# The tail of layer 3's query and key splits moved from VectorE to GpSimd, and the planner's tables replaced

## What is computed

```
for each of 4 layers:
    x = x + gate * out(self_attention(norm(x) * scale + shift))
    x = x + gate * out(cross_attention(norm(x) * scale + shift, context))
    x = x + gate * mlp(norm(x) * scale + shift)
```

## Time and profile before

| | before |
|---|---|
| median of 3 runs | 2908.7 us (2907.26 to 2917.39) |
| the profiled execution | 2916.84 us |
| its span, first to last instruction | 2915.0 us |
| instructions | 47676 |
| mean granted TensorE clock | 0.976 of full speed |
| DVE busy | 65% |
| ACT busy | 49% |
| POOL busy | 20% |

### The profile page before, as it was taken

The page is one execution under the profiler, slowest core; times in us unless marked ns, Lnnn a source line. Parts: engine busy times, 40 slices in busy tenths (PEclk is TensorE's granted clock), DMA queues, the critical chain, the costliest instruction groups (busy, mean ns, idle before and its releaser), DMA issues. The chain is left out here.

```text
span 2915.0 us, 47676 instructions
## 1 busy us (share of the span) xinstructions
PE 2728.5 (94%) x15136; PEld 1351.8 (46%) x15136; DVE 1893.7 (65%) x4209; ACT 1425.8 (49%) x2579; POOL 590.3 (20%) x999
## 2 busy tenths in 40 slices
PE   8999999999989999999988888898999999999899
PEld 5444344335544424334455566656645323224456
DVE  5977388642574783866344889668974884885621
ACT  3455635574445583566644444333221674785441
POOL 2110001131331110331125323411020010112510
PEclk9999999999999999999998999999999999999899
DMA  6333122433452312233066516521420322123621
GB/s 207 69 104 107 41 72 71 112 89 98 144 172 53 114 51 67 91 115 95 22 186 186 167 50 195 146 85 60 147 60 1 116 60 52 45 61 108 183 92 38
DMA packets 268153, 286.78 MB, mean 98 GB/s; under 512 B 70665, under 2 KB 207243, under 8 KB 267275
## 3 DMA queue, kind: packets, MB, share of 16 engines
q1 hardware_dynamic: 256651, 282.28, 33.0%
q0 software_dynamic: 11264, 1.46, 0.3%
HBM read 167.43 MB, written 114.72 MB: 97 GB/s over the span
## 5 line engine op out<-in xcount | busy, mean ns | idle before, releaser
L1570 ACT ACTIVATE probs<-ring_b 128x512 f32<-128x512 f32 (+1 forms) x1728 | 921.8, 599 | 457.9 <-PE ring_b L1429 359.9
L1748 DVE TENSOR_REDUCE row_max<-ring_a 128x1 f32<-128x1024 f32 x512 | 602.0, 1218 | 151.7 <-PE ring_a L1385 150.9
L1429 PE MATMUL ring_b<-q_ring,k_ring 100*128 100x512 bf16 x1536 | 526.8, 381 | 10.5 <-ACT probs L1570 2.8
L1385 PE MATMUL ring_a<-k_ring,q_ring 96*128 96x512 bf16 x1536 | 450.1, 383 | 27.9 <-DVE row_max L1748 16.1
L1462 PE MATMUL ring_c<-probs,v_and_ones 128*17 128x512 f32 x3072 | 402.0, 599 | 1.8 <-ACT probs L1570 1.2
L1745 DVE CUSTOM_DVE_ANT_0 w_mlp<-ring_a,w_mlp 128x1024 bf16<-128x1024 f32 x256 | 302.1, 1222 | 49.6 <-PE ring_a L1385 48.4
L1868 POOL CAST neg_max_parts<-neg_max 16x128 bf16<-16x128 f32 x112 | 37.6, 336 | 1392.1 <-ACT neg_max L1564 1141.3
L1429 PEld LDWEIGHTS ring_b<-q_ring,k_ring 100*128 100x128 bf16 x1536 | 145.7, 97 | 349.9 <-issue 241.5
L1385 PEld LDWEIGHTS ring_a<-k_ring,q_ring 96*128 96x128 bf16 x1536 | 135.5, 98 | 250.5 <-issue 153.6
L1485 PE MATMUL ring_b<-h_feat,w_mlp 128*128 128x512 f32 x512 | 230.3, 595 | 1.4 <-ACT h_feat L1541 0.8
L1497 PE MATMUL ring_a<-w_mlp 128*128 128x256 f32 x1024 | 226.1, 380 | 5.0 <-DVE w_mlp L1803 2.4
(11 more groups left out here) (143 smaller groups left out, 3346.4 us busy)
## 6 DMA issues: line engine op xcount, KB each, us to landing
q_ring<-scr_q SPq DMA_DIRECT2D x128, 384.0 KB, 4.3
scr_q<-split SPq DMA_DIRECT2D x64, 384.0 KB, 2.6
k_ring<-scr_k SPq DMA_DIRECT2D x64, 384.0 KB, 5.0
scr_q<-split SPq DMA_DIRECT2D x64, 256.0 KB, 3.0
scr_out<-out_stage SPq DMA_DIRECT2D x128, 128.0 KB, 2.5
scr_out<-out_stage SPq DMA_DIRECT2D x64, 256.0 KB, 2.4
h_feat<-scr_out SPq DMA_DIRECT2D x56, 256.0 KB
reciprocals<-scr_recip SPq DMA_DIRECT2D x56, 256.0 KB
```

The source lines that it names most:

```text
L1385: last = mm(ps[:, half * BLOCK:(half + 1) * BLOCK], q[0:PARTS, h, t * P:(t + 1) * P], k_view(g)[0:PARTS, h, half * BLOCK:(half + 1) * BLOC ...
L1429: last = mm(ps[:, :], k_view(g)[0:ROWS, h, s.kt * P:(s.kt + 1) * P], q[0:ROWS, h, q0:q0 + BLOCK], start=not g.masked, stop=True)
L1570: f(PT[0:n, s.pt, :], ps[0:n, :], ACT.Exp, **kw).then_inc(b_evac, 1)
L1748: v.tensor_reduce(NM[:, s.nm, s.u:s.u + 1], ps, AX.X, ALU.max).then_inc(a_evac, 1)
```

## The change

Three things. In layer 3 (`TAILS = (3,)`) a rotated split becomes two steps: `rotate` (PE and the first four DVE instructions) and `tail` (three GpSimd instructions, the same arithmetic), with a semaphore from DVE to POOL and one from POOL to whoever waits for the split. The splits of the context's keys stay as they were. The DMAs of the maxima stay on POOL's queue, as before. And all tables that set the order (`RANK`, `SECOND`, `LATER`, `REACH`, `DELAY`) have new numbers, so that the order changes in all layers, mostly by a few places.

```diff
-REACH = dict(PE=0.0, ACT=0.0, DVE=0.05, POOL=0.0, SP=0.2)
-DELAY = (7.5, 100)
+REACH = dict(PE=0.0, ACT=0.05, DVE=0.0, POOL=0.8, SP=0.2)
+DELAY = (7.5, 7.5)
-    tk=(10.1, 0.1, -12, 9.9),
+    tk=(-7, -12, -12, -11),
...
+TAILS = (3,)
...
-        d = yield do("split", ([("PE", 0.264 if ck else 0.86)] if rope else []) + [("DVE", (2.08 if rope else 0.84) if ck else 4.3 if rope else 1.79)],
-                     after=[s], ring="a" if rope else None, counts=["split_n"], of=s, rope=rope, l=l)
+        if rope and l in TAILS and not ck:
+            t = yield do("rotate", [("PE", 0.86), ("DVE", 2.55)], after=[s], ring="a", counts=["turned_n"], of=s, l=l)
+            d = yield do("tail", [("POOL", 3.5)], after=[t], counts=["tail_n"], of=s, turned=t, l=l)
+        else:
+            d = yield do("split", ([("PE", 0.264 if ck else 0.86)] if rope else []) + [("DVE", (2.08 if rope else 0.84) if ck else 4.3 if rope else 1.79)],
+                         after=[s], ring="a" if rope else None, counts=["split_n"], of=s, rope=rope, l=l)
...
+                        if s.kind == "rotate":
+                            v.tensor_copy(parts[:, 0, :], r).then_inc(turned, 1)
...
+                elif s.kind == "tail":
+                    f = s.of
+                    r = RAW[:, f.raw, 0:f.width]
+                    parts = SPLIT[:, f.split, :, 0:f.width]
+                    pool.wait_ge(turned, s.turned.turned_n + 1)
+                    link(g_.tensor_tensor(out=r, in0=r, in1=parts[:, 0, :], op=ALU.subtract))
+                    link(g_.tensor_copy(parts[:, 1, :], r))
+                    g_.tensor_tensor(out=parts[:, 2, :], in0=r, in1=parts[:, 1, :], op=ALU.subtract).then_inc(tail_done, 1)
```

More of the change, by code:

```diff
@@ L283 @@
 RANK = dict(
[L284 to L295, removed]
-    tk=(10.1, 0.1, -12, 9.9),
-    tk_s=(-0.5, 6.1, -9.2, -5.2),
-    win_f=(-6, -12, -4, 0),
-    win_s=(10.5, 8.5, 7.5, 6.5),
-)
-REACH = dict(PE=0.0, ACT=0.0, DVE=0.05, POOL=0.0, SP=0.2)
-DELAY = (7.5, 100)
[L303 to L306, removed]
+    init=(13.7, 1.2, -5.8, 1.9),
+    mod=(10.8, 10.8, -3.2, 11.1),
+    prep=(12.3, -9, -2.9, -2.9),
+    out=(0, -10, -8, -10),
+    ctx=(8.3, -6.7, 10.3, -6.7),
+    load=(24, 1.8, -10, 1.8),
+    cross_f=(-6.9, 10.8, 2.1, 3.1),
+    cross_s=(7.7, 3.8, 8.9, 12.9),
+    mlp=(-1, -1, -1, 0),
+    self_f=(-3, 24, 23, 20),
+    self_pv=(22, 24, 22, 24),
+    self_s=(-11, 1.1, -12, 3.1),
+    tk=(-7, -12, -12, -11),
+    tk_s=(6.7, -0.9, -12, 6.7),
+    win_f=(5.8, 8.5, -2.9, -8),
+    win_s=(6.2, 0.5, 4.5, -4.4),
+)
+REACH = dict(PE=0.0, ACT=0.05, DVE=0.0, POOL=0.8, SP=0.2)
+DELAY = (7.5, 7.5)
+SECOND = dict(init=24, mod=-23, prep=-3, out=3, ctx=16, load=-11, cross_f=20,
+              cross_s=15, mlp=-11, self_f=-4, self_pv=12, self_s=-1, tk=-13, tk_s=-3,
+              win_f=-22, win_s=20)
+LATER = (-9, -5.5, -6, -28)
 FILL_ONE = 0.11
+TAILS = (3,)
 def rank_of(kind, l, b, blk):
@@ L996, in blocks_kernel, with split_ended @@
         xn_ready, ctxn_ready = sem("xn_ready"), sem("ctx_norm_ready")
-        split_done = sem("split_done")
+        split_done, turned, tail_done = sem("split_done"), sem("rotated"), sem("tail_done")
+        def split_ended(eng, d):
+            if d.kind == "tail":
+                eng.wait_ge(tail_done, d.tail_n + 1)
+            else:
+                eng.wait_ge(split_done, d.split_n + 1)
         scr_in = [sem(f"scratch_written_{i}") for i in range(SPLITS)]
@@ L1153, in _ @@
                         elif r.kind == "scratch":
-                            sp.wait_ge(split_done, r.done.split_n + 1)
+                            split_ended(sp, r.done)
                         elif r.kind == "ctx_put":
@@ L1163, in _ @@
                     d, s = s.done, s.of
-                    sp.wait_ge(split_done, d.split_n + 1)
+                    split_ended(sp, d)
                     for j, parts in SCRATCH[s.which[-1]]:
@@ L1344, in _ @@
                     last.then_inc(b_full, 1)
-                elif s.kind == "split" and s.rope:
+                elif s.kind == "rotate" or s.kind == "split" and s.rope:
                     f = s.of
@@ L1550, in _ @@
                         else:
-                            act.wait_ge(split_done, s.raw_last.split_n + 1)
+                            split_ended(act, s.raw_last)
                     col = {"q": 4 if s.cross else 0, "k": 2, "ck": 6}[s.which] + s.hh
@@ L1676, in _ @@
                     v.tensor_tensor(GB[:, 0, :], ps[:, 0:FEAT], ROWS_IN[:, s.row.slot, :], ALU.add).then_inc(a_evac, 1)
-                elif s.kind == "split":
+                elif s.kind in ("split", "rotate"):
                     f = s.of
@@ L1680, in _ @@
                     parts = SPLIT[:, f.split, :, 0:f.width]
-                    if s.rope:
+                    if s.kind == "rotate" or s.rope:
                         dve.wait_ge(tables_in, 16 * 3)
```

12 lines of the change are left out of this document (7 added, 5 removed).

## The result

The changed kernel took 2922.1 us (median of 15 runs, 2913.1 to 2935.8); the kernel before took 2910.1 us in the 15 runs beside it (2904.9 to 2920.9). The ratio is 1.0041, 95% interval 1.0026 to 1.0055: some 12 us slower. The forecast was 2901 against 2908.7, 7.4 us faster, with a range to 2920.

What follows compares the result with a forecast made beforehand. PE is busy 94% of the span, but DVE was taken to bound layer 3's top-k stretch and latency chains its cross attention. Terms -11.8 - 2 + 6.4 = -7.4 us on the median 2908.7 gave 2901.3; range 2886 to 2920.

Steps and rivals of the forecast that it cites:

- In all earlier layers the count is 613 and 614: 0: Before layer 3's preparation: almost unchanged filler count on PE, so no change in time, bounds -4 and +4 us.
- a change in layers 0 and 1: Sign named in advance that would show the forecast wrong: any change in these first layers.
- The transition: DVE-bound stretch of item b's layer 3 top-k: eight tails off DVE win 14.3 us, lock costs 2.5, sum -11.8 us.
- The lock of the tails: DVE and POOL blocking each other at the first split's tail in the top-k stretch: 2.5 us, bounds 0 and 3.2.
- Rival C: Slower: DVE loses to POOL's tails in the top-k stretch; with all eight meeting the lock +18 us, 2926; chance 0.16.
- the sign that L1703 would stand at its usual 0.69 but for one place: In layer 3's top-k stretch, this DVE instruction keeps its usual time at all places except one.
- Eight (item b's) lie where PE is the limit: 0: Item b's eight self attention tails in layer 3: hidden behind PE, so moving them changes nothing, 0 us.
- The other orders: First top-k scores to layer 3's first rotation: 28 fillers fewer; -2 us taken, bounds 0 and -3.9; earlier layers 0.
- Cross attention: Layer 3: first maxima queue on POOL behind four tails, scores 8.5 us late, 2 won back; net +6.4, bounds 0 and 13.
- A: The forecast itself, 2901 us: transition and cross attention both behave as summed; chance 0.38.
- the four rivals: The forecast's cases: as summed 2901 (chance 0.38), faster 2891 (0.28), slower 2926 (0.16), nothing to measure about 2909 (0.18).

Runs made afterwards that it cites:

- E1: The changed kernel with the second number of DELAY raised from 7.5 to 30, so item b's layer norms become ready later: ratio 0.9999 to the kernel before.
- E3: The changed kernel in its own order, only the transfer of item b's first 512 rows of x issued earlier, right behind item a's: ratio 1.0005 to before.
- E2: The kernel before with DELAY=(7.5, 7.5) in place of (7.5, 100) and nothing else: ratio 1.007 to before, 20 us slower.
- E5: The changed kernel in its own order, all tails done by DVE in the place of their rotations: ratio 1.0097 to before, 16 us over the changed kernel.
- E10: E1 with the planner taking the maxima transfer of item a's first layer 3 group 12 us longer: ratio 0.9996, against 0.9999 for E1.
- E9: Code of after, tables of before, self attention tails alone on POOL, planned to keep before's DVE and POOL order: ratio 0.9966, 2904.1 us against 2914.7.
- E12: The kernel before's order word for word, with all 24 tails put into POOL's order afterwards: ratio 0.9988 to before, against 0.9966 for E9.
- E8: The changed kernel with DELAY=(7.5, 30) and tails on POOL in self attention alone, planned anew: ratio 1.0003 to before.
- E13: E1 in its own order, the eight cross attention tails done by DVE in place of their rotations: ratio 1.0007 to before, against 0.9999 for E1.
- E4: The changed kernel with tails on POOL in layer 3's self attention alone, cross attention planned anew without them: ratio 1.0027 to before.
- E11: The changed kernel with its new tables but TAILS=(), planned anew with no tail on POOL: ratio 1.0075 to before, 22 us slower.
- E6: Code of the changed kernel with all tables of before, tails in self and cross attention, planned anew: ratio 1.0033 to before, 10 us slower.

## Why the prediction was wrong, by its own steps

**The step that failed** is "In all earlier layers the count is 613 and 614: 0". It rests on a count of fillers, and fillers stand only where the planner foresees a wait. In the plan the first statistics of an item wait for nothing but `DELAY` (their `src` is None, the load of x is no step), so the plan of after has item b's at 7.5 us, where the chip had them at 21.1. It has PE's first transposes at 13.0 us, with 16 fillers ahead of them, where the plan of before has them at 12.4 with 12; the chip had them at 26.4. So the count could not show the wait. In before the number in `DELAY` was 100, which kept item b's statistics far behind the landing of its x. By E1 and E3 this costs 10 to 12 us in after, more than the whole forecast; E2 has the same stall in the order of before. With it repaired, the kernel is 0.9999 of before. The prediction had named "a change in layers 0 and 1" as a sign of being wrong, and that is what came.

**The transition**, forecast -11.8, measured -10.7 in the whole change, -8.3 in the order of before and -13.8 in that of after. Mechanism and size were right. The lock of the tails was forecast at one place and 2.5 us. It is at that place:

```profile
2026.54 1.58 POOL L1873 TENSOR_TENSOR raw<-raw,split 128x512 f32<-128x512 f32 x1 [4.79 <-DVE split L1707]
2027.62 1.05 DVE L1703 TENSOR_TENSOR raw<-raw,rope_or_context 128x512 f32<-128x512 f32 x1
2028.18 0.95 POOL L1874 CAST split<-raw 128x512 bf16<-128x512 f32 x1
2028.70 0.98 DVE L1705 TENSOR_TENSOR raw<-raw,split 128x512 f32<-128x512 f32 x1
2029.21 1.48 POOL L1875 TENSOR_TENSOR split<-raw,split 128x512 bf16<-128x512 f32 x1
2029.71 1.27 DVE L1707 CAST split<-raw 128x512 bf16<-128x512 f32 x1
```

Each engine is drawn out in turn, DVE's cast from 0.43 to 1.27 us; all eight splits together lose 1.4 us, so the place was right and 2.5 too high. By the Trainium skill (SBUF — State Buffer, section "SBUF: two separate sides") whoever comes second waits until the other's instruction has ended; the rows agree: L1703, begun at 2027.62, ends at 2028.67, some 0.55 us behind POOL's end at 2028.12, and so in turn. Rival C, the lock at all eight, did not come. But the sign that L1703 would stand at its usual 0.69 but for one place failed, for a reason that isn't the tails:

```profile
2060.68 1.22 POOL L1907 TENSOR_TENSOR topk_scores<-topk_scores,topk_first 128x616 f32<-128x616 f32 x1 [9.10 <-DVE topk_marks L1783]
2061.06 1.40 DVE L1703 TENSOR_TENSOR raw<-raw,rope_or_context 128x512 f32<-128x512 f32 x1
```

Three of the eight L1703 stand beside this subtraction of the top-k in the order of after (1.33 to 1.40 us each, with the tails on DVE too, E5), one of eight in before. That is some 1.4 us, as much as the tails lose, and it came with the order.

**"Eight (item b's) lie where PE is the limit: 0"** is right in the order of before (379.8 and 380.0 us) and open in that of after, where E5 is 6 us longer with the tails on DVE, for a reason that no run sets apart.

**The other orders**, forecast -2. The top-k stages scatter too much for a term of that size (366.0 to 375.6 us in one order). What was not seen is the order behind the last mask and in self attention, together +4.7 us in after and 4.4 with E1; E10 shows that these two stages can't be read apart, and which steps of the order cost them is open.

**Cross attention**, forecast +6.4. The last stage of after is 8 us longer than in the execution before, and the means of the two orders are 9 apart: the size was near. The wait is where it was put (8.5 less 2 is 6.5 and not 6.4, which changes nothing). The timeline of after, first scores:

```profile
2704.52 1.07 PE L1429 MATMUL ring_b<-q_ring,ctx_keys 100*77 100x512 bf16 x2 [3.71 <-DMA q_ring<-neg_max_parts]
```

That is 49.8 us behind item a's statistics (2654.7) where the earlier trace rows has 39.3 (2683.00 less 2643.7), so over 10 us late; 8.5 was worked out. But two causes were taken as one. Each alone: the tails cost some 6.4 us in the order of before (E9, E12), and nothing that can be measured in that of after (E1, E8, E13), whose loss is the order itself. The late first scores go with both splits of a block standing ahead of the first maxima: E4, E8 and E11, planned without tails there, have them at 48.7 to 48.8 us, and E6, with tails but its first maxima ahead of the second block's rotations, at 40.6. How much of the stage hangs on that is not shown: E6 has the longest last stage of all, and E3, with scores at 48.2, has a last stage of 268.4 us, where before has 268.0. So the near size of this term was in part luck: its queue of tails on POOL was the smaller part.

**The sum.** With the start taken out (E1) the ratio is 0.9999, where -7.4 us would be 0.9975. The stages of after say -10.7 + 4.7 + 8.0 = +2 us for transition, what lies behind it, and cross attention; E1's interval is -4 to +3 us. So A had its two places right and lacked two terms, 4.7 us behind the mask and 12 at the start, and none of the four rivals had looked at the start.

## What to carry to other kernels

A count of planned waits is evidence only about what the plan knows: before such a count is used, look for loads that no step waits for, and read the first instruction of each engine against the landing of its data. When a change comes with a new order, freeze the order and move the work alone: here the move of self attention's tails was worth -10 us (E9), and the new order took more than that. A plan's gain in one stage should be taken together with the next, as work may only have crossed the border between them.

## What the runs showed of the hardware

A tail on POOL is 1.7 times as long as on DVE (3.1 and 1.81 us), and DVE loses 1.4 us over eight tails, at the one that stands beside a rotation; beside MAX and MATCH_REPLACE it loses nothing that shows (MAX8 takes 222 to 223 ns, and 225 to 226 with the tails on DVE). L1703 takes 0.68 us alone and 1.33 to 1.40 beside the top-k subtraction of POOL. The transition, where DVE is full, repeats to 0.1 us over seven executions of different kernels (116.5), while the last stage of one order took 261.9, 262.8, 265.6 and 268.0 us; a single profile can't carry a term of 5 us there. A stall at the start was worth 12 us in one order (E1) and 20 us in the other (E2), with the same 10 us on PE's first transpose; that difference is not explained.
